# Narrow attention of a two-layer ViT tower on one core: mixing with undivided probabilities and tokens on partitions, mixed heads transposed one step later, and the first stage's weight loads issued from SyncE

## The reference

```python
qkv = (x @ w_qkv).reshape(B, N, 3, H, 16)                 # H = 12 heads, N = 36 tokens
a = softmax(einsum('bhnd,bhmd->bhnm', q, k) * 0.25 (+ bias), axis=-1)
o = einsum('bhnm,bhmd->bhnd', a, v)                       # mixing of the values
y = x + o.reshape(B, N, 192) @ w_proj + b_proj
```

## Time and profile before

| what | us |
|---|---|
| median of 3 runs | 901.41 |
| lowest and highest | 895.21, 904.11 |
| the profiled execution, its own time | 900.14 |
| its span, first to last instruction | 898.4 |

### The profile page before, as it was taken

The page is one execution under the profiler, slowest core; times in us unless marked ns, Lnnn a source line. Parts: engine busy times, 40 slices in busy tenths (PEclk is TensorE's granted clock), DMA queues, the critical chain, the costliest instruction groups (busy, mean ns, idle before and its releaser), DMA issues. The chain is left out here.

```text
span 898.4 us, 21351 instructions
## 1 busy us (share of the span) xinstructions
PE 824.2 (92%) x7767; PEld 744.7 (83%) x7767; DVE 540.4 (60%) x1467; ACT 440.0 (49%) x1094; POOL 409.6 (46%) x489
## 2 busy tenths in 40 slices
PE   9889999999999799997999989898979999999983
PEld 8889998899998577776999987777757899899973
DVE  2226555465566788885673326989976622466645
ACT  0346565456554376764345525756636221355533
POOL 1544544354444444443432217867851455244445
PEclk9989999999999999997899998999979999999997
DMA  9810111011110131213500003733200011333243
GB/s 313 263 50 13 28 38 36 27 30 36 33 42 2 33 58 32 30 25 101 102 1 1 1 2 67 146 64 68 44 6 1 32 64 62 82 99 99 81 157 112
DMA packets 103942, 55.78 MB, mean 62 GB/s; under 512 B 67264, under 2 KB 94512, under 8 KB 103840
## 3 DMA queue, kind: packets, MB, share of 16 engines
q1 hardware_dynamic: 98032, 43.04, 19.8%
q0 software_dynamic: 3792, 7.84, 2.5%
q10 hardware_dynamic: 2016, 3.54, 1.3%
HBM read 29.81 MB, written 13.97 MB: 49 GB/s over the span
## 5 line engine op out<-in xcount | busy, mean ns | idle before, releaser
L930 POOL TENSOR_TENSOR attn_prob<-attn_prob,attn_recip 100x432 f32<-100x432 f32 x64 | 58.5, 914 | 69.3 <-DVE attn_recip L1313 69.1
L450 POOL TENSOR_TENSOR attn_prob_x<-attn_prob,attn_recip 100x864 f32<-100x864 f32 x32 | 52.6, 1644 | 52.7 <-DVE attn_recip L759 52.7
L1889 POOL DMA_INDIRECT results<-moe_hid_shared x43 | 41.2, 959 | 58.5 <-ACT moe_hid_shared L2104 58.5
L1599 ACT ACTIVATE mlp_hid<-psum,columns 128x384 f32<-128x384 f32 x72 | 38.0, 579 | 41.5 <-PE psum L96 41.5
L1061 PEld LDWEIGHTS psum<-attn_prob_t,attn_values 108*64 108x64 f32 x1024 | 39.5, 142 | 14.3 <-ACT attn_prob_t L1180 8.9
L1061 PE MATMUL psum<-attn_prob_t,attn_values 108*64 108x36 f32 x1024 | 41.6, 228 | 7.6 <-ACT attn_prob_t L1180 4.6
L1173 ACT ACTIVATE attn_prob<-attn_prob 100x432 f32<-100x432 f32 x64 | 36.1, 564 | 20.7 <-POOL attn_prob L937 19.2
L2079 ACT ACTIVATE moe_silu<-psum 128x384 f32<-128x384 f32 x36 | 17.6, 490 | 56.6 <-PE psum L107 55.3
L1044 PE MATMUL psum<-ident,attn_prob 100*108 100x100 f32 x256 | 35.8, 265 | 8.4 <-POOL attn_prob L930 8.4
L436 POOL TENSOR_TENSOR attn_rstd<-attn_var_eps,neg_half 128x1 f32<-128x1 f32 x18 | 10.2, 568 | 71.3 <-DVE attn_var_eps L771 71.3
L1552 PE MATMUL psum<-mlp_w_dn_s,mlp_hid 128*128 128x192 f32 (+2 forms) x306 | 42.6, 290 | 0.0
(11 more groups left out here) (474 smaller groups left out, 2813.8 us busy)
## 6 DMA issues: line engine op xcount, KB each, us to landing
embed_patches<-in_x SPq DMA_DIRECT2D x8, 768.0 KB, 17.2
sorted_rows<-mlp_pad_zeros SPq DMA_DIRECT2D x1, 4214.0 KB, 15.6
moe_hid_shared<-sorted_rows SPq DMA_DIRECT2D x43, 98.0 KB, 1.9
attn_v<-attn_v_tok SPq DMA_DIRECT2D x16, 216.0 KB
attn_values<-attn_v_tok SPq DMA_DIRECT2D x96, 27.0 KB
side_raw_a<-in_w_gu_dram SPq DMA_DIRECT2D x8, 288.0 KB, 3.3
side_raw_b<-in_w_gu_dram SPq DMA_DIRECT2D x16, 144.0 KB, 3.4
h_rows<-results SPq DMA_DIRECT2D x6, 288.0 KB, 5.0
```

The costliest lines, as they stand in the source:

```text
L450: nc.gpsimd.tensor_tensor(prob_x[k % 2][:, :, :, :], prob[k % 3][:, :, :].rearrange("p h (a n) -> p h a n", a=1) .to_broadcast([QP, HEADS, ...
L930: nc.gpsimd.tensor_tensor(pr, pr, recip[k % 2][:, :].rearrange("p (h a) -> p h a", a=1) .to_broadcast([QP, HEADS, SEQ]), ALU.mult).then_in ...
L1599: nc.scalar.activation(hid_step(n), bank(n % 3)[:, 0:MW], ACT.Gelu, bias=b_up[:, c:c + 1]).then_inc(S["gelu_done"], 1)
L1889: nc.gpsimd.indirect_dma_start(out=results, out_offset=bass.IndirectOffsetOnAxis(ap=x_in[j % x_ring][:, D:D + 1].bitcast(U32), axis=0), in ...
```

## The change

In the narrow stages the probabilities are no longer divided. `values_bd` gets a seventeenth column per head that holds ones, so the mixing yields the sum of each head's row beside its 16 channels. Mixing swaps its operands: the transposed exponentials are stationary and the values move, so the result has tokens on partitions (100 x 204). DVE takes the reciprocal of the sums and multiplies (`norm_z`), PE transposes the result in two pieces of 102 columns (`turn_z`) one step later, and ACT copies them to z_t. `sum_up` and POOL's `normalise` are gone. `turn` moves from step k+2 to step k+1 and `mix` from step k+3 to step k+2; `turn_z`, `copy_z` and all behind stay where `mix` and `copy_z` were. The values are laid out as 64 floats (16 channels of four heads, interleaved) in one run of 256 bytes; DMA counts and partitions are unchanged. Scores use 36 query columns per image where they used 64, and fit two PSUM banks. The ones are made by two affine selects per values buffer.

In the embedding, SP issues the four weight loads between the batches of patches; ACT's waits for batches are gone. DVE's `following.split` moves one tile earlier and `scale_columns` before the last tile.

```diff
-            if 1 <= k <= units:
-                normalise(k - 1)
...
-            for a in range(3):
...
-                    to = values_bd[g % 2][SEQ * j:SEQ * j + SEQ, 3 * a:3 * a + n, :].rearrange(
-                        "p i (m n) -> p (i m) n", m=4)[:, :, 16 * j:16 * j + 16]
-                    of = v_tok[SEQ * a:SEQ * a + SEQ, j, 0:n, :].rearrange("p i (m n) -> p (i m) n", m=4)
+                    at = 4 * HW * j
+                    to = values_bd[g % 2][SEQ * j:SEQ * j + SEQ, 3 * a:3 * a + n, at:at + 64]
+                    of = v_tok[SEQ * a:SEQ * a + SEQ, j, 0:n, :]
...
+            for n in range(4):
+                both = prob_t[k % 2][:, n, :, :].rearrange("p a q -> p (a q)")
+                for a in range(2):
+                    i = 2 * u + a
+                    v = values_bd[g % 2][:, 3 * (i % 3) + i // 3, :].rearrange("p (e n) -> p n e", n=4)[:, n, :]
...
+                    last = nc.tensor.matmul(z_ps[to, 3 * HW * n:3 * HW * (n + 1)], both[:, toks], v,
+                                            start=True, stop=True)
+        def turn_z(k):
+            pe.wait_ge(S["z_normed"], k + 1)
...
             if k >= 3:
-                mix(k - 3)
+                turn_z(k - 3)
+            if 2 <= k < units + 2:
+                mix(k - 2)
...
-            if 2 <= k < units + 2:
-                turn(k - 2)
+            if 1 <= k <= units:
+                turn(k - 1)
...
-        def sum_up(k):
...
+        def norm_z(k):
+            dve.wait_ge(S["mixed"], k + 1)
+            z = z_ps[0:QP, :].rearrange("p (h e) -> p h e", h=HEADS)
+            nc.vector.reciprocal(recip[k % 2][:, :], z[:, :, 16]).then_inc(S["recip_ready"], 1)
...
+            nc.vector.tensor_tensor(z_tok[k % 2][:, :, :], z, recip[k % 2][:, :].rearrange("p (h a) -> p h a", a=1)
+                                    .to_broadcast([QP, HEADS, HW]), ALU.mult).then_inc(S["z_normed"], 1)
```

More of the change, by code:

```diff
@@ L1033, in scores @@
                 at = u * UNIT + a * SEQ
[L1034 removed]
+                last = nc.tensor.matmul(scores_ps[64 * a:64 * a + m, 1], q_b[g % 2][:, at:at + m],
                                         keys_b[g % 2][:, :, at:at + SEQ], start=True, stop=True)
@@ L1053, in mix @@
             if k >= 1:
-                pe.wait_ge(S["z_copied"], k)
[L1055 to L1063, removed]
+                pe.wait_ge(S["z_normed"], k)
+            for n in range(4):
[3 more added lines that the diff above has]
+                    v = values_bd[g % 2][:, 3 * (i % 3) + i // 3, :].rearrange("p (e n) -> p n e", n=4)[:, n, :]
+                    m = 64 if k == 0 and a == 0 else SEQ
+                    toks, to = slice(a * SEQ, a * SEQ + m), slice(64 * a, 64 * a + m)
+                    last = nc.tensor.matmul(z_ps[to, 3 * HW * n:3 * HW * (n + 1)], both[:, toks], v,
+                                            start=True, stop=True)
+            last.then_inc(S["mixed"], 1)
+        def turn_z(k):
+            pe.wait_ge(S["z_normed"], k + 1)
+            if k >= 1:
+                pe.wait_ge(S["z_copied"], k)
+            flat = z_tok[k % 2][:, :, :].rearrange("p h e -> p (h e)")
+            for c in range(2):
+                last = nc.tensor.transpose(bank(5)[0:ZC, c * P:c * P + QP], flat[:, c * ZC:(c + 1) * ZC],
+                                           ident[0:QP, 0:QP])
+            last.then_inc(S["z_turned"], 1)
         def project_out(t):
@@ L1345, in vector @@
                 take_scores(k)
-            if 1 <= k <= units:
-                sum_up(k - 1)
+            if 2 <= k < units + 2:
+                norm_z(k - 2)
             if j == 0 and g + 1 < groups:
@@ L2466, in _ @@
             load(5)
+            load_one(sp, S, stage_a, stage_b, jobs, 0)
+            load(6)
             load_pos(2, 6)
-            load(6)
+            load_one(sp, S, stage_a, stage_b, jobs, 1)
+            load(7)
+            load_one(sp, S, stage_a, stage_b, jobs, 2)
+            load(8)
             prep["load_columns"](sp)
-            for n in range(7, len(batches)):
-                load(n)
+            load_one(sp, S, stage_a, stage_b, jobs, 3)
+            load(9)
             prep["load"](sp)
@@ L2885, in by_group @@
         v = np.asarray(v)
-        out = np.zeros((2, 2, 4, 16) + v.shape[1:], v.dtype)
-        out[:, :, 0:3] = v.reshape((2, 2, 3, 16) + v.shape[1:])
-        return out.reshape((2, P) + v.shape[1:])
+        out = np.zeros((2, P) + v.shape[1:], v.dtype)
+        heads = v.reshape((2, HB, 16) + v.shape[1:])
+        for h in range(HB):
+            out[:, HW * h:HW * h + 16] = heads[:, h]
+        return out
     def narrow_columns(w):
```

117 lines of the change are left out of this document (55 added, 62 removed).

## The result

| | us |
|---|---|
| before, median of 4 runs (one more than shown above) | 902.43 |
| after, median of 4 runs | 915.10 (913.02 to 917.41) |
| ratio after to before | 1.0143, 95% interval 1.0104 to 1.0182 |
| after, the profiled execution, its own time and its span | 913.02, 910.9 |

The change makes the kernel 1.4% slower. Forecast were 904, with a range of 882 to 920.

What follows compares the result with a forecast made beforehand. PE was taken as nearest to the bound, beside a value-DMA loop of almost the same length. Embedding -6.0, attn2 +4.4, attn3 +0.1, clock +5.1 and mixing 0 gave +3.6 on 900.14, so 904 us, range 882 to 920.

Steps and rivals of the forecast that it cites:

- likeliest case: Whole kernel: the forecast's own sum of 904 us, with 896 to 911 for it alone; chance 0.50.
- rival D: Narrow stages: reading moving values at a stride of four floats doubles the mixing's 0.61 us; 917 us, chance 0.10.
- The mixing itself, about 0: Narrow stages: swapped mixing plus turn_z changes a unit by -0.10 to +0.42 us; taken as 0, with -6 to +6.
- turn_z, 0.17: Narrow stages: two added transposes per unit cost 0.17 us, half of the 0.34 that four take.
- sum_up and normalise gone: POOL and DVE work dropped: 0 in regular groups, -1 at attn2's end, -5 at attn3's, -1.5 in one attn3 group.
- mix one step earlier: Wait for values moves to a group's third step, loop floor 14.7 us: +4.4 in attn2, +0.1 in attn3.
- The issues at their length: SP's nine value DMAs per group stay at 7.5 us with 256-byte runs, some 0.82 each.
- Rival B: Value DMAs with 256-byte runs issue in 0.52 us each, so values come earlier; 882 us, chance 0.22.
- The embedding, -6.0: Embedding's end: barrier at 42.4 instead of 46.2 us, -3.8, and attn1 starting at full clock, -2.2.
- rival E: Embedding: its edit gives nothing, weights among the patches delay them or land as late; 910 us, chance 0.05.
- Clock, +5.1: Narrow stages: two longer waits in attn3 and one regular group each get a half-clock stretch costing 1.7 us.
- rival C: Narrow stages: each group's wait for values drops the clock, eleven more stretches of 1.7 us; 922 us, chance 0.13.

Runs made afterwards that it cites:

- e6: Changed kernel with the moving values contiguous through the order of the weights' columns, ScalarE's copies unchanged; 915.23 us, ratio 1.0143 to the kernel before.
- e4: Changed kernel with turn_z issued twice; 920.67 us, ratio 1.0175 to the kernel before.
- e3: Changed kernel with five of a group's nine value DMAs, four blocks of values left out; 906.05 us, ratio 1.0025 to the kernel before.
- e12: Changed kernel, values still strided, with the mixing one step later; 899.59 us, ratio 0.9965 to the kernel before.
- e13: e11 with SP asking for the last batch of patches before the fourth weight matrix; 891.76 us, ratio 0.9856 to the kernel before.
- e1: Kernel before with the changed embedding alone; 903.32 us, ratio 0.9996 to the kernel before.
- e5: Changed kernel with 64 instead of 36 query columns in the scores; 914.76 us, ratio 1.0136 to the kernel before.
- e2: Changed kernel with contiguous moving values, reordered by ScalarE's copies in nine instructions a group instead of three; 923.11 us, ratio 1.0211 to the kernel before.
- e7: e6 with four of a group's nine value DMAs issued on ScalarE's queue; 945.81 us, ratio 1.0479 to the kernel before.
- e9: e6 with five of a group's nine value DMAs, four blocks of values left out; 890.34 us, ratio 0.9875 to the kernel before.
- e11: e6 with all nine value DMAs and the mixing one step later; 889.60 us, ratio 0.9878 to the kernel before.

## Why the prediction was right and wrong

The time lies in the range, but above the likeliest case's own (896 to 911). It came near the 917 of rival D, and by D's cause. That the range held it is in part luck: three terms of the sum were wrong. The mixing and the embedding were put too low and the clock too high, and these errors offset one another in part.

*The mixing itself, about 0: wrong, and the step that cost most.* For a unit the prediction had -0.10 to +0.42 us, 27 in all at most. Measured are 0.30 for the mixing and 0.31 for turn_z, 0.61 together and 39 us in 64 units, above the upper bound. And between its bounds it took 0, on the ground that only a mixing or two per group stand in the loop. This fails twice. In the loop the stretch behind the waiting mixing was left at 5.87 us and came out as 6.85, so the floor is 15.56 and not 14.7. Outside of it TensorE was busy for 12.82 of 13.75 us, and nobody added the new work to that: with the upper bound it is 12.82 + 4 x 0.42 = 14.50, close under the floor of 14.7, and with what was measured 12.82 + 4 x 0.61 = 15.26, against 15.27 in the trace.

*The reason for 0.85: rival D, not the columns.* The 0.86 worked out by the columns lies near it by chance. D put the mixing at over 1 us; e6 shows 0.49 without the stride and 0.85 with it. It is a factor of 1.7, 64 x 0.36 = 23 us of TensorE's time. The Trainium skill ("SBUF — State Buffer", section "Specifications (TRN2)") states that each crossing to a new line of 16 bytes pays a penalty, and gives no size for it. The runs agree with it: 0.85 us where each column lies in a new line, 0.49 where they are contiguous. I gave D a chance of 0.10 and priced it in the loop alone (13.4); it stands in the loop and in TensorE's whole work.

*turn_z, 0.17: half of what it holds PE for.* The marginal pair costs 0.17 (e4), but a block of two in its place holds PE for 0.31.

*sum_up and normalise gone: right.* norm_z's multiplication takes 0.371 us where 0.37 was worked out. L1332's 3.18 us have no match after: the same operation (L1347) has a mean of 630 ns against 835.

*mix one step earlier: right as a mechanism, too short as a floor.* The floor of 14.7 is seen in e6 as 14.96, and the wait at attn3's start came as 2.96 us. In the changed kernel the loop takes 15.56, since the strided mixings and turn_z stand in it; TensorE's own work, seen with the loop eased (e3), is 15.25. The early mixing costs: e12 against the changed kernel is 15.5 us by the medians.

*The issues at their length: right.* They take 7.49 us with runs of 256 bytes and with runs of 64 (e6). Rival B is out.

*The embedding, -6.0: wrong.* The barrier did not move. I had written that SP has only patches behind the weight loads, and those were what counted: PE waits 1.79 and 1.12 us for patches that SP asks for later than before. Whether the wait for a free staging buffer or the transfers themselves made them late stays open (e13). Of the -6.0 only the 2.2 us of attn1 at full clock are seen in the stages, and by e1 rival E (0.05) is nearest, with nothing left in the total.

*A misreading.* In the group the prediction has ACT busy for 10.82 us and POOL for 10.12. The first is PEld's number and the second ACT's; POOL is busy for 4.95. In the same way the 5.89 us of ACT at 45.60 are PEld's, and ACT has 1.99. It entered the choice of -2.2 for attn1's start, and 2.2 us is what came; the other terms do not rest on it.

*Clock, +5.1: wrong in sign.* Half-clock stretches went from ten with 66.4 us to five with 30.2. One of 6.8 us went with the embedding's edit, and at the MLP's start 13.6 us became 6.8, which goes with the MLP's 2.5 us less. In the narrow stages a TensorE with more to do stood idle less. Of the waits for values only that of 2.96 us was followed by such a stretch. Those of 0.23 to 1.40 us were not, so rival C is out. The idle times at attn3's end, with their stretch at 660.0 to 670.3, are gone, and that goes with attn3 growing less than attn2 (+4.4 against +11.8).

Together: TensorE's further work in 64 units, 64 x 0.61 = 39 us, partly filled idle time that was there, and the stalls and half-clock stretches that went paid for more. +12.5 in the span is what is left. The size of each of these shares was not measured.

## What to carry to other kernels

Before costing an edit on the engine that is busiest, add it to that engine's busy time in the regular group and compare the sum with every other floor; two bounds within 5% of each other hide each other, and each experiment that eases only one will say that it was not the cause (here 0 and 9 us alone, 25 together). Added work can stand in both: count it in the engine's total and again in every loop that passes through it. Lay out a matmul's moving operand so that its columns are contiguous, even where, as here, that makes the DMA runs shorter. An engine with a third of its time idle is no place for DMA issues if it stands in every unit's chain.

## What the runs showed of the hardware

- Moving fp32 columns at a stride of 16 bytes: eight matmuls of 36 stationary by 51 moving columns take 0.85 us (after, e3, e4, e5, e12), contiguous 0.49 to 0.50 (e2, e6, e7, e9, e11, e13).
- A DMA of 36 partitions takes 0.78 us to issue on SP's queue, and the next starts 0.82 us after it, whether its runs are 64 or 256 bytes long (medians in before, after and e6). On ScalarE's queue four take 3.25 to 4.4 us in e7, 3.49 in the rows shown, and no instruction of ScalarE starts meanwhile.
- Single issues are longer at times: the nine behind load_down took 8.75 us before, 10.9 in e6, 11.6 in e1 and 12.4 in e11, where TensorE then waited 3.95 us. What lengthens them stays open.
- Narrowing the scores' stationary operand from 64 to 36 columns takes six fp32 matmuls from 0.80 (e5) to 0.76 us (after).
- The length of a wait of TensorE alone does not tell whether half clock follows. A wait of 1.80 us at 300.33 in the kernel after has no such stretch behind it; one of 1.81 at 302.12 in e12 has one from 302.6 to 309.4.
